# The last feed-forward part's down products in three products of rounded parts, made by ScalarE and GpSimd

## The chip, the cores and the metric

One core of a Trainium2 chip. Its engines are TensorE (PE in the profile; PEld is its weight load), VectorE (DVE), ScalarE (ACT), GpSimd (POOL) and SyncE (SP, which here only starts DMAs). The metric is the device time of one execution in microseconds, lower is better.

## The reference

A block of four layers over x (8 batches of 256 tokens, width 256): causal attention with 16 heads, a mixture of 64 experts with two shared experts, an mLSTM layer, and a feed-forward layer with 2:4 pruning. Each is `x = x + layernorm(layer(layernorm(x)))`. The change is in the last one:

```python
def _sparsify_2to4(h):                       # of each 4 neighbours the 2 of largest magnitude stay
    g = h.reshape(B, S, I // 4, 4)
    _, idx = jax.lax.top_k(jnp.abs(g), 2)
    ...
h = jax.nn.silu(x @ w_gate) * (x @ w_up)     # w_gate, w_up: 256 x 1024
return _sparsify_2to4(h) @ w_down            # w_down: 1024 x 256
```

## The kernel before

The 2048 tokens lie on 16 tiles of 128 rows. Every engine runs its own list of instructions in order, and the lists are held together by semaphores (`wait_ge`, `then_inc`); what stands behind a waiting instruction on its engine waits too. The layers follow one another, with some overlap at the borders.

The last feed-forward part works in 32 steps (`STEPS`): 4 units `u` of 512 tokens, in each 8 blocks `n` of 128 hidden columns (`NI`), i = 8u + n. The hidden columns are laid out so that the four neighbours of a pruning group fall into four blocks following each other, so pruning is done over four steps 4q to 4q+3 at a time, elementwise between whole blocks.

- TensorE, `hidden(i)`: gate and up products into PSUM banks S, 512 columns wide. The weights and the inputs are already split in rounded parts: `three` (lines 959 to 961) makes a product as high x high + high x low + low x high in the float32r type. That is 12 products a step. `down2(i)` multiplies the pruned block i with its 128 rows of w_down, four tiles of 128 tokens by 256 columns, in plain float32 (line 1518; the trace has two records for each of these). In TensorE's list `down2(i - 6)` follows `hidden(i)`. `down_last` takes the last four blocks: first two of the four token tiles for all four blocks, then the other two.
- ScalarE: `silu(i)` reads the gate bank (line 914); `magnitudes(i)` takes the absolute values (line 920). In its list step i is `magnitudes(i)`, `silu(i + 1)`.
- VectorE: `product(i)` multiplies silu and up into `hb[:, i % 8]` (line 2176). Pruning: `order_pair` (lines 2183, 2184; in the steps with i % 4 = 3 and 0), `compare_pairs` (2189, 2190; i % 4 = 0), `tallies` (2194, 2195) and the first two `sparsify` (2202) with i % 4 = 1, the last two `sparsify` with i % 4 = 2. So block 4q is pruned in step 4q+5, and TensorE multiplies it after `hidden(4q+6)`.
- The residual of a unit: in steps n = 6 and 7 of the next one `unit_stats` takes the moments from PSUM (lines 1558, 1561), `unit_residual` normalises (1566) and adds (2230), in step n = 7 for the first half and in step n = 0 of the one after for the second. The factor 1/sqrt(variance + eps) comes from GpSimd (`ln_event`, lines 446 and 447, into `veps` and `rstd`); VectorE waits for it. `last_rows` puts the output and residual of the mLSTM layer's last batch into the steps 0 to 10; it needs two more of these events, "out" for step 6 and "res" for step 8.
- GpSimd has nothing else in this part than these nine events, in a plain row.

The earlier feed-forward part (the shared experts of the mixture) already works with rounded hidden parts: ScalarE's `hidden_high` copies, rounded, GpSimd's `low_hidden` (line 466) or VectorE subtracts, and `rows_down` multiplies with `three`.

```python
for i in range(STEPS + 6):               # TensorE
    if 2 <= i < STEPS:
        hidden(i)
    ...
    if 6 <= i < STEPS + 2:
        down2(i - 6)
down_last()
```

Of the kernel before, what the change touches and what calls it, by code (L numbers as in the profile page):

```python
# [6 lines left out]
ALU = mybir.AluOpType  # L7
# [47 lines left out]
def build(nc, io, out):  # L55
    ctx = ExitStack()
    with ctx:
# [131 lines left out]
                  for i in range(2))  # L189

        lastw = parts[:, 0:NI * 2 * BW].rearrange("p (n k w) -> p n k w", n=NI, k=2)
        ordered = raw[:, :, 0:2 * KC * P]

# [246 lines left out]
        def _(pool):  # L441
            ch = Chain(pool, s["pool_c"])

            def ln_event(event, cp, n=2):
                pool.wait_ge(s["ln_mv"], event + 1)
                cp(pool.tensor_scalar(veps[:, 0:n], mv[:, 0:n, 1], LN_EPS, None, ALU.add))  # L446
                pool.tensor_tensor(rstd[:, 0:n], veps[:, 0:n], mhalf[:, 0:n], ALU.pow).then_inc(s["ln_rs"], 1)  # L447
# [171 lines left out]
                    gather_rows(b + 3, (5, 6, 7))  # L619
                    shared_row(b + 3)  # L620
            base += 4 * NB
            ln_event(ln_at["out", NB - 1], cp)
            ln_event(ln_at["res", NB - 1], cp)
            for k in range(2 * NUNIT - 1):
                ln_event(base + k, cp, 4 if k == 2 * NUNIT - 4 else 2)

        @block.scalar
        def _(act):
# [286 lines left out]
            def magnitudes(i):  # L916
# [2 lines left out]
                    act.wait_ge(s["d_cmp"], (i - 4) // 2 + 1)  # L919
                act.activation(ab[:, i % 4, :], hb[:, i % 8, :], ACT.Abs).then_inc(s["d_abs"], 1)  # L920

            silu(0)
            for i in range(STEPS):
                magnitudes(i)
                if i == 2:
                    head_rows_copy(NB)
                if i + 1 < STEPS:
                    silu(i + 1)
                if i == 9:
                    final_input_copy(NB - 1)  # L930

# [2 lines left out]
        def _(pe):  # L934
# [565 lines left out]

            def down2(i):
                u, n = divmod(i, NI)
                pe.wait_ge(s["d_hs"], i + 1)
                if i == 0:
                    pe.wait_ge(s["w_down"], 32)
                    pe.wait_ge(s["c_hc"], NB)
                if i == NI:
                    pe.wait_ge(s["c_xall"], NB + 1)
                if n == 0 and u >= 2:
                    pe.wait_ge(s["d_x"], u - 1)  # L1510
                for t in range(4):
                    last = down_tile(i, t)
                last.then_inc(s["d_dn"], 1)

            def down_tile(i, t):
                u, n = divmod(i, NI)
                bank, o = ROWS[2 * ((u + 1) % 2) + t // 2], (t % 2) * D
                last = pe.matmul(bank[:, o:o + D], hb[:, i % 8, t * P:(t + 1) * P], down_rows[n // RING][:, n % RING, :],  # L1518
                                 start=n == 0 and t % 2 == 0, stop=n == NI - 1, skip_group_check=True)
                if n == NI - 1 and t == 1:  # L1520
                    last.then_inc(s["d_half"], 1)
                return last

            def down_last():
                for half in range(2):
                    for i in range(STEPS - 4, STEPS):
                        if half == 0:
                            pe.wait_ge(s["d_hs"], i + 1)
                        for t in (2 * half, 2 * half + 1):
                            last = down_tile(i, t)  # L1530
                        if half:
                            last.then_inc(s["d_dn"], 1)
# [17 lines left out]
        def _(dve):  # L1550
# [620 lines left out]
            def product(i):  # L2171
                dve.wait_ge(s["d_sg"], i + 1)
                dve.wait_ge(s["d_u"], i + 1)
                if i >= 8:
                    dve.wait_ge(s["d_dn"], i - 7)
                dve.tensor_tensor(hb[:, i % 8, :], sgl[i % 2], S[2 + i % 2][:], ALU.mult).then_inc(s["d_h"], 1)

            def order_pair(q, p):
# [162 lines left out]
```

## Time and profile before

| | us |
|---|---|
| median of 3 runs (lowest, highest) | 975.22 (974.08, 975.96) |
| the profiled execution: span from its first to its last instruction | 1017.7 |
| TensorE busy in it | 862.2 (85%) |
| VectorE busy | 667.7 (66%) |
| GpSimd busy | 396.7 (39%) |
| ScalarE busy | 389.5 (38%) |

The profile is of one execution, and no time of it as a whole is shown beside its span; the span is 42 us above the median of the runs. Times in the rows are us from the start of the span. A timeline row gives start, duration, engine, source line, operation, output and inputs by tile name, shape, the number of instructions merged in it, and in brackets how long the engine had been idle and what ended that. The last feed-forward part lies between 848 and 1012 us.
### The profile page before, as it was taken

What the parts mean: (1) busy time and instruction counts of PE and PEld (TensorE: products, weight loads), DVE (VectorE), ACT (ScalarE), POOL (GpSimd) and SP (SyncE); (2) the same over time, 40 slices, a digit from 0 to 9 for tenths busy, and PEclk for the clock granted to TensorE, in tenths of its full rate; (3) what the DMA queues carried; (4) which work ended last, traced back from release to release, by engine and by line L of the source; (5) the groups of instructions that cost most, each with busy time, mean ns of one, the idle gap of its engine ahead of it and who ended that gap; (6) DMA issues with size and microseconds to landing.
All of it is one profiled execution on the core that took longest, in us unless ns stands there. A gap on an engine that the chain in (4) does not pass through costs nothing.

```text
span 1017.7 us, 18542 instructions
## 1 busy us (share of the span) xinstructions
PE 862.2 (85%) x6718; PEld 722.4 (71%) x6718; DVE 667.7 (66%) x1500; ACT 389.5 (38%) x764; POOL 396.7 (39%) x548
## 2 busy tenths in 40 slices
PE   4899899898688857667777859899999999999994
PEld 3777777776576846556666748778788888788883
DVE  6567777765577615885444547668778865867875
ACT  2244444444433713232222325435555564222220
POOL 3123333323432266766565283466665322100001
PEclk9799999998899968998898977758888887999997
DMA  7000000000000248888876551221111000000001
GB/s 248 2 1 13 12 12 9 5 12 12 22 1 22 87 136 260 250 257 242 242 222 184 162 178 52 82 59 52 46 42 41 0 1 1 0 1 21 22 1 41
DMA packets 59384, 77.66 MB, mean 76 GB/s; under 512 B 9746, under 2 KB 51997, under 8 KB 59304
## 3 DMA queue, kind: packets, MB, share of 16 engines
q1 hardware_dynamic: 32040, 40.92, 13.1%
q0 software_dynamic: 9856, 18.92, 6.9%
q10 hardware_dynamic: 17408, 16.78, 4.7%
q8 instruction: 47, 0.77, 0.3%
q14 instruction: 33, 0.27, 0.1%
HBM read 61.88 MB, written 23.07 MB: 83 GB/s over the span
## 4 chain that ended last, share of the span: by engine, by line
PE 43%; DVE 12%; issue 5%; another core or an unknown queue 4%; ACT 3%; POOL 2%; DMA 1%; ACTq 0%; POOLq 0%; DVEq 0%
PE S L1310 5%; PE S L1298 4%; PE S L959 3%; PE S L961 3%; PE S L960 3%; PE S L944 3%; PE ZO L1518 2%; PE ZO L1321 2%; PE T L1321 2%; PE T L1518 2%; PE ZO L1431 2%; DVE work L1566 1%; PE ZO L1433 1%; PE ZO L1432 1%
## 5 line engine op out<-in xcount | busy, mean ns | idle before, releaser
L529 POOL DMA_INDIRECT work<-xnd,rows_at x128 | 134.8, 1053 | 87.6 <-issue 38.6
L446 POOL TENSOR_SCALAR veps<-mv 128x2 f32<-128x2 f32 (+1 forms) x63 | 15.6, 247 | 287.8 <-DVE mv L1561 287.6
L1999 DVE TENSOR_TENSOR work<-work,S 64x256 f32<-64x256 f32 x128 | 54.2, 424 | 83.0 <-ACT work L798 52.9
L455 POOL TENSOR_SCALAR_AFFINE_SELECT work<-work 128x256 f32<-128x256 f32 x128 | 53.7, 444 | 118.0 <-ACT work L650 118.0
L959 PE MATMUL ZO<-parts 128*128 128x256 f32 x224 | 71.4, 319 | 16.6 <-DVE parts L1600 6.4
L959 PE MATMUL S<-xr,parts 128*128 128x512 f32 x192 | 83.5, 435 | 0.8 <-issue 0.8
L960 PE MATMUL S<-xr,parts 128*128 128x512 f32 x192 | 77.5, 404 | 0.0
L961 PE MATMUL S<-xr,parts 128*128 128x512 f32 x192 | 77.5, 403 | 0.0
L782 ACT ACTIVATE work<-S 128x512 f32<-128x512 f32 x64 | 38.2, 597 | 100.7 <-PE S L1298 43.5
L650 ACT ACTIVATE work<-S 128x768 f32<-128x768 f32 x64 | 51.7, 812 | 55.5 <-PE S L1033 55.5
L960 PE MATMUL ZO<-parts 128*128 128x256 f32 x224 | 66.3, 296 | 0.0
L961 PE MATMUL ZO<-parts 128*128 128x256 f32 x224 | 66.2, 295 | 0.0
L1033 PE MATMUL S<-parts 32*128 32x256 f32 (+1 forms) x768 | 57.9, 288 | 4.8 <-DVE parts L1626 3.8
L959 PEld LDWEIGHTS ZO<-parts 128*128 128x128 f32 x224 | 45.3, 202 | 21.9 <-issue 9.3
L1310 PE MATMUL S<-work,raw 128*128 128x128 f32 x296 | 46.7, 309 | 10.8 <-issue 10.7
L545 POOL DMA_INDIRECT attn_w<-yd,slots x44 | 49.8, 1131 | 11.9 <-issue 11.9
L1298 PE MATMUL S<-ident,work 128*128 128x128 f32 x256 | 47.4, 314 | 8.2 <-DMA work<-xnd,rows_at 8.2
L1033 PEld LDWEIGHTS S<-parts 32*128 32x128 f32 x768 | 48.9, 191 | 7.1 <-DVE parts L1626 5.0
L1310 PEld LDWEIGHTS S<-work,raw 128*128 128x128 f32 x296 | 42.5, 221 | 13.0 <-issue 12.9
L447 POOL TENSOR_TENSOR rstd<-veps,mhalf 128x2 f32<-128x2 f32 (+1 forms) x63 | 48.1, 763 | 5.2
L798 ACT ACTIVATE work<-S 64x256 f32<-64x256 f32 x64 | 24.1, 377 | 59.1 <-remote 30.8
L960 PEld LDWEIGHTS ZO<-parts 128*128 128x128 f32 x224 | 45.8, 205 | 0.1
(330 smaller groups left out, 2355.7 us busy)
## 6 DMA issues: line engine op xcount, KB each, us to landing
yd<-work ACTq DMA_DIRECT2D x64, 256.0 KB
raw<-in_experts SPq DMA_DIRECT2D x74, 192.0 KB
work<-in_experts SPq DMA_DIRECT2D x36, 192.0 KB
lg_all<-in_experts SPq DMA_DIRECT2D x18, 192.0 KB
xnd<-attn_w SPq DMA_DIRECT2D x8, 256.0 KB, 2.1
shd<-work SPq DMA_DIRECT2D x8, 256.0 KB, 2.3
work<-xnd,rows_at POOLq DMA_INDIRECT x128
raw<-in_ffn SPq DMA_DIRECT2D x2, 1024.0 KB, 5.4
```

The costliest lines, as they stand in the source:

```text
L447: pool.tensor_tensor(rstd[:, 0:n], veps[:, 0:n], mhalf[:, 0:n], ALU.pow).then_inc(s["ln_rs"], 1)
L455: last = pool.affine_select(out=diagonal, in_=diagonal, compare_op=ALU.is_ge, fill=0.0, base=0, pattern=[[0, 2], [1, P]], channel_multipli ...
L529: pool.indirect_dma_start(xg[:, i % RING, b, :], None, xnd[:], bass.IndirectOffsetOnAxis(ap=rows_at[:, 2 * i + b:2 * i + b + 1], axis=0), ...
L545: pool.indirect_dma_start(gathered(b, t, k), None, yd[:], bass.IndirectOffsetOnAxis(ap=slots[:, 2 * b + t, k:k + 1], axis=0)).then_inc(s[" ...
L650: act.activation(pt[n % 6], SS[:, at:at + 1024].rearrange("p (r x) -> p r x", r=2)[:, :, 0:384], ACT.Exp).then_inc(s["a_exp"], 1)
L959: pe.matmul(dst, a(0), b(0), start=start, stop=False, skip_group_check=True)
L960: pe.matmul(dst, a(0), b(1), start=False, stop=False, skip_group_check=True)
L961: return pe.matmul(dst, a(1), b(0), start=False, stop=stop, skip_group_check=True)
L1033: return pe.matmul(bank[:, 2 * half * P:(2 + half) * P], side, top, start=k == 0 and half == 0, stop=k == 2, skip_group_check=True)
L1298: last = pe.transpose(S[i % 2][:, o:o + P], xg[:, i % RING, b, c * P:(c + 1) * P], ident[:])
L1310: last = pe.matmul(S[2 + i % 2][:, b * P:(b + 1) * P], pair_weights(i)[:, o:o + P], xT[:, i % 2, b, c, :], start=(c == 0), stop=(c == KC - 1))
L1999: last = dve.tensor_tensor(hx[64 * half:64 * half + 64, i % 2, :], sgx[64:128, i % 2, :], S[2 + i % 2][64:128, 0:256], ALU.mult)
```

## The change

The down products are made by `three` from rounded parts, too. The parts of the eight weight blocks are made once, at the start (`down_high` on ScalarE, `down_low` on GpSimd). The parts of each pruned block are made by `kept_high` (ScalarE, a copy into float32r) and `kept_low` (GpSimd, the block less its high part), in a ring of four. TensorE waits for the low part (`f_hl`) instead of for the pruned block (`d_hs`), and VectorE's `product(i)`, which writes over block i-8, waits for the low part of that block instead of for its down product. The layer norm events on GpSimd are put between the `kept_low` of the steps.

```diff
+        last_down = lastw[:, :, :, 2 * KC * P:BW]
+        last_hidden = parts[:, NI * 2 * BW:].rearrange("p (m k t) -> p m k t", m=4, k=2)
@@ gpsimd @@
-            ln_event(ln_at["out", NB - 1], cp)
-            ln_event(ln_at["res", NB - 1], cp)
-            for k in range(2 * NUNIT - 1):
-                ln_event(base + k, cp, 4 if k == 2 * NUNIT - 4 else 2)
+            def down_low(n):
+                pool.wait_ge(s["f_wh"], NSH + NI + n + 1)
+                pool.tensor_tensor(last_down[:, n, 1], down_rows[n // RING][:, n % RING, :], last_down[:, n, 0],
+                                   ALU.subtract).then_inc(s["f_wl"], 1)
+
+            def kept_low(i):
+                pool.wait_ge(s["f_hh"], NQ * NJ + i + 1)
+                pool.tensor_tensor(last_hidden[:, i % 4, 1, :], hb[:, i % 8, :], last_hidden[:, i % 4, 0, :],
+                                   ALU.subtract).then_inc(s["f_hl"], 1)
+
+            for n in range(NI):
+                down_low(n)
+            for i in range(STEPS + 3):
+                q, j = divmod(i, 4)
+                u, n = divmod(i, NI)
+                if q and j in (1, 2):
+                    kept_low(4 * q + 2 * j - 6)
+                    kept_low(4 * q + 2 * j - 5)
+                if i == 5:
+                    ln_event(ln_at["out", NB - 1], cp)
+                if i == 6:
+                    ln_event(ln_at["res", NB - 1], cp)
+                if 0 < u < NUNIT - 1 and n >= 6:
+                    ln_event(base + 2 * (u - 1) + n - 6, cp)
+                if i == STEPS - 1:
+                    ln_event(base + 2 * (NUNIT - 2), cp, 4)
+            for k in range(2):
+                ln_event(base + 2 * NUNIT - 3 + k, cp)
@@ scalar @@
+            def down_high(n):
+                act.wait_ge(s["w_down"], 16 * (n // RING + 1))
+                act.activation(last_down[:, n, 0], down_rows[n // RING][:, n % RING, :], ACT.Copy).then_inc(s["f_wh"], 1)
+
+            def kept_high(i):
+
+                act.wait_ge(s["d_hs"], i + 1)
+                if i >= 4:
+                    act.wait_ge(s["d_dn"], i - 3)
+                act.activation(last_hidden[:, i % 4, 0, :], hb[:, i % 8, :], ACT.Copy).then_inc(s["f_hh"], 1)
+
             silu(0)
-            for i in range(STEPS):
-                magnitudes(i)
+            for i in range(STEPS + 3):
+                q, j = divmod(i, 4)
+                if i < STEPS:
+                    magnitudes(i)
                 if i == 2:
                     head_rows_copy(NB)
                 if i + 1 < STEPS:
                     silu(i + 1)
+                if i < 4:
+                    down_high(2 * i)
+                    down_high(2 * i + 1)
+                if q and j in (1, 2):
+                    kept_high(4 * q + 2 * j - 6)
+                    kept_high(4 * q + 2 * j - 5)
@@ tensor, down2 @@
-                pe.wait_ge(s["d_hs"], i + 1)
+                pe.wait_ge(s["f_hl"], NQ * NJ + i + 1)
+                if i < NI:
+                    pe.wait_ge(s["f_wl"], NSH + NI + i + 1)
@@ tensor, down_tile @@
-                last = pe.matmul(bank[:, o:o + D], hb[:, i % 8, t * P:(t + 1) * P], down_rows[n // RING][:, n % RING, :],
-                                 start=n == 0 and t % 2 == 0, stop=n == NI - 1, skip_group_check=True)
+                last = three(bank[:, o:o + D], lambda k: last_hidden[:, i % 4, k, t * P:(t + 1) * P],
+                             lambda k: last_down[:, n, k], n == 0 and t % 2 == 0, n == NI - 1)
@@ tensor, down_last @@
-                            pe.wait_ge(s["d_hs"], i + 1)
+                            pe.wait_ge(s["f_hl"], NQ * NJ + i + 1)
@@ vector, product @@
-                    dve.wait_ge(s["d_dn"], i - 7)
+                    dve.wait_ge(s["f_hl"], NQ * NJ + i - 7)
```

## Rows read from the trace of the kernel before

**Rows 1.** Busy time by stretch: us, busy (records) by engine, granted clock, DMA

```profile
870.00:980.00 110.00, 108.08 (x478) 89.11 (x477) 84.76 (x151) 29.74 (x49) 6.91 (x12) 1.00 0.03 10
```

**Rows 2.** TensorE's timeline, steps 9 to 11: start, us, engine, line, tiles, records

```profile
891.99 1.89 PE L1518 MATMUL ZO<-lg_all,work 128*128 128x256 f32 x8
896.52 1.89 PE L1518 MATMUL ZO<-lg_all,work 128*128 128x256 f32 x8
```

**Rows 3.** TensorE's timeline, earlier feed-forward part in three products

```profile
588.54 0.29 PE L959 MATMUL ZO<-parts 128*128 128x256 f32 x1
...
589.99 0.40 PE L959 MATMUL S<-xr,parts 128*128 128x512 f32 x1
...
592.79 0.28 PE L959 MATMUL ZO<-parts 128*128 128x256 f32 x1
```

**Rows 4.** Timeline of VectorE and ScalarE, steps 9 and 10

```profile
887.65 0.69 DVE L2176 TENSOR_TENSOR work<-work,S 128x512 f32<-128x512 f32 x1
...
889.58 1.29 DVE L2202 SCALAR_TENSOR_TENSOR work<-attn_w,work 128x512 f32<-128x512 bf16 x2
...
890.79 0.60 ACT L914 ACTIVATE work<-S 128x512 f32<-128x512 f32 x1 [1.79 <-PE S L961]
```

**Rows 5.** ScalarE's groups by line and shape: count, busy us, mean ns

```profile
L715 ACT ACTIVATE parts<-work 128x512 fp32r<-128x512 f32 x16 | 10.1, 632 | 25.8 <-DVE work L1736 22.6 <-issue 3.2
```

**Rows 6.** GpSimd's subtraction of the earlier part, line 466: ns minimum/median/maximum

```profile
L466 POOL TENSOR_TENSOR parts<-work,parts x12: 1262/1296/2841, 283.0 to 344.2; 128x512 fp32r<-128x512 f32 x12
```

**Rows 7.** Timeline of VectorE and GpSimd where the two meet

```profile
292.87 1.23 DVE L1773 TENSOR_TENSOR lg_all<-lg_all,work 128x1024 f32<-128x1024 f32 x1
292.97 2.27 POOL L466 TENSOR_TENSOR parts<-work,parts 128x512 fp32r<-128x512 f32 x1 [5.05 <-ACT parts L715]
294.13 2.19 DVE L1776 TENSOR_TENSOR work<-lg_all,rbias 128x1024 f32<-128x1024 f32 x1
```

**Rows 8.** GpSimd's timeline, one layer norm event of the last part

```profile
913.29 0.22 POOL L446 TENSOR_SCALAR veps<-mv 128x2 f32<-128x2 f32 x1 [34.34 <-DVE mv L1561]
913.60 0.72 POOL L447 TENSOR_TENSOR rstd<-veps,mhalf 128x2 f32<-128x2 f32 x1
```

**Rows 9.** VectorE's timeline over one unit, steps 13 to 21

```profile
905.94 0.69 DVE L2176 TENSOR_TENSOR work<-work,S 128x512 f32<-128x512 f32 x1 [0.42 <-PE S L961]
...
914.88 0.69 DVE L2176 TENSOR_TENSOR work<-work,S 128x512 f32<-128x512 f32 x1 [1.68 <-ACT work L914]
...
917.29 0.99 DVE L1566 TENSOR_SCALAR work<-ZO,mv,rstd 128x256 f32<-128x256 f32 x2
...
928.11 1.29 DVE L2202 SCALAR_TENSOR_TENSOR work<-attn_w,work 128x512 f32<-128x512 bf16 x2
...
942.87 0.69 DVE L2176 TENSOR_TENSOR work<-work,S 128x512 f32<-128x512 f32 x1 [0.41 <-PE S L961]
```

**Rows 10.** Busy time by stretch around two pauses of TensorE, with its granted clock

```profile
258.50:260.30 1.80, 0.06 (x1) 0.00 (x0) 0.44 (x1) 1.80 (x5) 1.67 (x4) 1.00 0.42 146
260.30:262.00 1.70, 1.68 (x40) 1.25 (x44) 0.00 (x0) 1.70 (x3) 1.66 (x1) 1.00 0.04 10
272.90:276.00 3.10, 0.00 (x0) 0.00 (x0) 1.89 (x8) 0.00 (x0) 0.94 (x2) 1.00 0.00 0
276.00:278.00 2.00, 1.95 (x7) 1.75 (x8) 0.76 (x2) 0.80 (x2) 0.00 (x0) 0.50 0.38 131
```

**Rows 11.** Timeline of TensorE and VectorE in the tail

```profile
996.83 10.21 PE L1518 MATMUL T<-lg_all,work 128*128 128x256 f32 x32 [2.96 <-DVE work L2202]
...
1003.62 0.76 DVE L1558 BATCH_NORM_STATS2 st<-T 128x6 f32<-128x256 f32 x2 [1.65 <-PE T L1518]
...
1007.70 0.76 DVE L1558 BATCH_NORM_STATS2 st<-T 128x6 f32<-128x256 f32 x2
```

**Rows 12.** Timeline of TensorE and VectorE, down product 0 and the last output's normalisation

```profile
873.35 1.99 PE L1518 MATMUL ZO<-raw,work 128*128 128x256 f32 x8 [0.93 <-DVE work L2202]
...
874.41 0.99 DVE L1566 TENSOR_SCALAR work<-T,mv,rstd 128x256 f32<-128x256 f32 x2
```

More of the change, by code:

```diff
@@ L1502, in down2 @@
                 u, n = divmod(i, NI)
-                pe.wait_ge(s["d_hs"], i + 1)
+                pe.wait_ge(s["f_hl"], NQ * NJ + i + 1)
+                if i < NI:
+                    pe.wait_ge(s["f_wl"], NSH + NI + i + 1)
                 if i == 0:
-                    pe.wait_ge(s["w_down"], 32)
                     pe.wait_ge(s["c_hc"], NB)
```

## Prediction

> **What bounds the kernel now.** I read the busy shares by stretch first, then TensorE's timeline, then VectorE's and ScalarE's around the places where TensorE takes up a down product. In the last feed-forward part TensorE is busy for 108.08 of 110 us, at full clock; VectorE for 84.76, ScalarE for 29.74 and GpSimd for 6.91 [rows 1]. So TensorE sets the time there, and a shorter down product would pay, if nothing new comes between. One step (hidden unit i of 32: 12 products of 512 columns for gate and up, then the down product of unit i-6) takes 896.52 - 891.99 = 4.53 us [rows 2]. The earlier feed-forward part has the changed form of the step already: 12 products of 256 columns take 589.99 - 588.54 = 1.45 us, and 12 of 512 take 592.79 - 589.99 = 2.80 us [rows 3]. So the down product costs 4.53 - 2.80 = 1.73 us now.
>
> **TensorE's gain.** The rounded form costs 1.45 us instead of 1.73: 0.28 us for each of 32 steps, 9.0 us in all, if every operand waits ready. A step becomes 4.25 us, four of them 17.0 us instead of 18.1.
>
> **The weights' parts.** Eight copies on ScalarE and eight subtractions on GpSimd, all before step 6. ScalarE is idle most of that time, so the copies cost nothing by themselves; without that cover they would be eight times less than 0.63 us. The subtractions are charged below, with the start.
>
> **The hidden units' parts.** 32 copies on ScalarE (0.63 us each, by a copy of this shape [rows 5]) and 32 subtractions on GpSimd (median 1.30 us, 1.26 to 2.84 [rows 6]). Both engines have room. What counts is where they stand in line. Units are pruned four at a time: VectorE finishes the first two in step 4q+1 and the others in step 4q+2, and TensorE wants the first one right after the 12 wide products of step 4q+2. In step 10 the pruned unit is there at 890.2 (889.58 and half of 1.29), TensorE takes it at 891.99. But ScalarE's new copy stands behind the silu of step 10, which runs from 890.79 to 891.39 [rows 4], 0.60 us before TensorE is free. Then 0.63 of copy, 0.07 to signal, 1.30 of subtraction, 0.07 to signal: 2.07 us after the silu, so TensorE waits 2.07 - 0.60 = 1.47 us. Once in four steps, in each group of four: 1.47 lost against 4 x 0.28 = 1.12 gained. The quiet groups lose 0.35 us each. The other three units have a whole step more and are ready. The wait for the ring of four, and VectorE's own (now for the subtraction instead of the down product), have long been met.
>
> **Contention.** At 292.97 a GpSimd subtraction meets a VectorE instruction with two SBUF inputs (292.87, 1.23 us) and takes 2.27 instead of 1.30; VectorE's next one, of the same size and kind, takes 2.19 instead of 1.23 [rows 7]. Each kept the other out for its whole length. All the pruning on VectorE is of this kind; its products of silu and up read PSUM and don't count. I therefore let a subtraction and a pruning instruction exclude each other; the other bound is that they don't. The Trainium skill, "SBUF — State Buffer", section "SBUF: two separate sides", states the same as a rule: the pair of ports is locked by the one that starts first, and the other blocks fully. By that rule the sum is the one with exclusion, and it speaks against this change; the trace agrees in the two instructions just read.
>
> **The groups with the layer norm.** In the last two steps of a unit of 8 (n = 6, 7) VectorE takes the moments of the unit before and waits for GpSimd's rstd, which is 0.22 + 0.72 us and some 1.0 us in all [rows 8]. The diff puts that event behind both subtractions of step n = 6. In the time of step 13's end of the wide products = 0: step 14's wait ends at 5.7, step 15's wide products at 9.95; ScalarE's silu of step 15 ends at 9.3, its two copies at 9.95 and 10.5, the subtractions run 10.0 to 11.3 and 11.3 to 12.6, or the second behind VectorE's ordering. VectorE's product is done at 10.8, but its three ordering instructions can't begin before 11.3 to 12.6 and take 1.9; rstd is there by 14.5 to 15.4. So the normalisation begins 4.3 to 5.2 us after the product's start at 10.2, where now it begins 917.29 - 914.88 = 2.4 after it [rows 9]. From there to the first pruned unit of the next group it is 928.11 + 0.65 - 917.29 = 11.5 us of VectorE's own work: 26.0 to 26.9. Copy, subtraction and signals: 28.0 to 28.9. TensorE's own work would bring it there at 0 + 5 x 4.25 + 1.47 = 22.7, so it waits 5.3 to 6.2 us. Eight steps then take 8 x 4.25 + 1.47 + 5.3 to 6.2 = 40.8 to 41.7 us, against 942.87 - 905.94 = 36.9 now: **3.9 to 4.8 us more, twice**. Without exclusion rstd is there at 13.6 and it is 2.9 more.
>
> **The clock.** A pause of 1.8 us left the granted clock at 1.00; after one of 3.1 us it was 0.50 through the 2 us that followed [rows 10], half of 2.4 GHz. The waits of 1.47 us should cost nothing more, those of 5 to 6 us should be followed by a stretch at half clock, on the path, since VectorE is ahead by then. Its price: at least 1.0 us (2 us at half speed), at most 3.3 (in the tail the first 16 of 32 records after a pause of 2.96 took 1003.62 - 996.83 = 6.79 us, the other 16 some 3.4 [rows 11]). I take 2.2, between them: **4.4 us for two**.
>
> **The start.** The weights' subtractions (half as wide as the hidden ones, by my estimate some 0.7 us each, from the 1.30 of [rows 6]) meet VectorE's ordering in steps 3 and 4 and hold it up by about the length of one, 0.65 us; copy, subtraction and signals add 2.0: down product 0 begins at 873.35 + 2.65 = 876.0. VectorE's normalisation of the last mLSTM output, at 874.41 now [rows 12], waits for a rstd that stands behind two subtractions: 876.0 + 1.3 + 0.95 = 878.2, 3.8 later. The next two subtractions hold the ordering of step 7 up for one more, and TensorE, paused for 3.6 us, is at half clock. I bring the product of step 9 to 892.4 instead of 887.65 [rows 4], the pruned unit to 895.0, down product 4 to 897.0 instead of 891.99: 5.0 us, or 4.3 without exclusion. Until step 13 three short down products and the shorter way to the product give 0.95 back: **3.4 to 4.1 us**.
>
> **The tail.** Nothing covers it. The last four units' copies and subtractions (4 x 1.3) stand behind the last pruning; TensorE's first half of the last down product ends 26.0 to 26.7 us after the wide products of step 29, where now it is 1003.62 - 979.6 = 24.0 [rows 11] (step 29 is one unit of 36.9 us after step 21, whose product starts at 942.87 [rows 9], 0.25 after its wide products). The second half is short again and the moments follow the normalisation, 1007.70 - 1003.62 = 4.1 later as now. **2.0 to 2.7 us**. VectorE's two older normalisations fit into the waiting.
>
> **The sum.** 3.8 + 2 x 4.3 + 4.4 + 2.3 = 19.1 us. The gain of 9.0 us is in it. Ends of the bounds: 3.4 + 5.8 + 2.0 + 1.5 = 12.7 with no exclusion and the smallest clock price; 4.1 + 9.6 + 6.6 + 2.7 = 23.0 with everything. The profiled execution has a span of 1017.7 us, the runs a median of 975.22: it is 42 us longer, and the trace doesn't say where. The stage repeats the same step evenly at full clock, so I carry the difference over unscaled: 975.2 + 19.1 = 994.3. Scaled by 975/1018 it would be 18.3.
>
> **Rivals.**
> 1. The forecast: waits, exclusion and clock, 15 to 23 us slower, 990 to 998. Chance 0.60.
> 2. Milder: the engines don't exclude each other or the clock stays up. 3.4 + 5.8 + 1.5 = 10.7 with neither, 19.1 - 4.4 = 14.7 with exclusion alone: 986 to 990. For it: only one meeting in the trace is unambiguous. Chance 0.20.
> 3. Harsher: a subtraction doesn't get in between VectorE's back-to-back instructions and takes 2.3 to 2.84 us, as two of 12 did [rows 6, 7]. About 1 us more in each of 7 groups: 998 to 1004. Against it: where VectorE waits for its own result there is a gap. Chance 0.10.
> 4. The other side: the way from silu to the low part is short enough. It decides at one place, copy plus subtraction behind the silu of step 4q+2: if they take less than 0.6 us instead of 2.07, TensorE never waits and keeps 9.0 us, less some 2 at the tail: 968. At 1.7 us it breaks even in the quiet groups. For it speaks only that GpSimd and ScalarE are mostly idle. Chance 0.05; that things cancel within 0.2% (about what a measurement of this kernel can tell from no change), 0.03.
>
> Slower by more than that: 0.60 + 0.20 + 0.10, and 0.02 for worse than rival 3: 0.92. Range for 8 in 10: 984 to 1002, from the lower end of the milder case to the middle of the harsher one.
>
> **What the changed profile would show.** Twelve records of 0.12 us in the place of eight of 0.216 in each down product. TensorE idle some 1.5 us before the first down product of a quiet group, released by GpSimd's subtraction; 5 to 6 us after the first steps of units 2 and 3, with a granted clock of 0.5 behind it. VectorE's ordering instructions stretched where a subtraction runs, its normalisation waiting for rstd. If TensorE's idle time before down products stays under 1 us, the forecast is wrong; if it is idle but at full clock, the clock term is; if the subtractions stay at 1.3 us and the ordering at 0.6, exclusion is.

## The result and the profile after

Four runs of the changed kernel took 992.98 us in the median (989.08 to 996.22), four of the kernel before 974.65 (973.73 to 975.96): ratio 1.0196, 95% interval 1.0159 to 1.0233. The change makes it 18.3 us slower; 994.3 in all and 19.1 more were forecast. The profiled execution took 991.72 us, with a span of 990.0.

The last part was 158.03 us long and is 176.74, from VectorE's `product(0)` to the end of its last residual addition. This table gives that time for all kernels of this study, cut at the products of steps 13, 21 and 29, each read from the starts of that instruction in VectorE's timeline. Runs of one kernel spread by up to 6 us either way. Much of that lies ahead of the last part: but for the 853.57 us of before, its first product starts anywhere from 803.08 to 816.38 us in these traces. The stretches of the table repeat to 0.1 us in many places where the work is the same (the first one of after, e2, e3 and e6, the units of e8, e12 and e13), so the verdicts below rest on them, and the runs stand beside. But where TensorE pauses for about 2 us or more, and its clock may fall, they do not all repeat so well: the two units, 13 to 21 and 21 to 29, hold the same work, and differ by 0.51 us in after, 0.86 in e3, 2.01 in e7 and 1.51 in e9. There is one trace of each kernel, so a difference of up to 2 us in such a unit or in the tail is not by itself the work of an edit. The last column compares with runs of the kernel before that were taken beside that kernel's, with medians of 973.87 to 974.66 us for the experiments.

| kernel | 0 to 13 | 13 to 21 | 21 to 29 | 29 to end | sum | runs, median | ratio to before, 95% interval |
|---|---|---|---|---|---|---|---|
| before | 52.37 | 36.93 | 36.97 | 31.76 | 158.03 | 974.65 | |
| after | 55.44 | 43.25 | 43.76 | 34.29 | 176.74 | 992.98 | 1.0159 to 1.0233 |
| e1_ready | 54.04 | 35.52 | 35.54 | 29.68 | 154.78 | 972.90 | 0.9966 to 1.0016 |
| e2_fill | 55.45 | 41.06 | 41.07 | 34.37 | 171.95 | 987.99 | 1.0106 to 1.0193 |
| e3_ln_first | 55.44 | 42.72 | 41.86 | 35.10 | 175.12 | 991.68 | 1.0117 to 1.0206 |
| e4_low_on_vector | 52.66 | 41.66 | 41.35 | 34.49 | 170.16 | 987.47 | 1.0084 to 1.0155 |
| e5_low_last | 54.29 | 40.82 | 40.89 | 33.20 | 169.20 | 986.97 | 1.0116 to 1.0179 |
| e6_residual_late | 55.45 | 41.89 | 42.46 | 35.99 | 175.79 | 991.12 | 1.0140 to 1.0216 |
| e7_all | 52.29 | 40.21 | 38.20 | 33.60 | 164.30 | 981.21 | 1.0051 to 1.0103 |
| e8_before_residual_late | 52.32 | 36.20 | 36.22 | 30.40 | 155.14 | 971.53 | 0.9956 to 1.0002 |
| e9_high_first | 52.28 | 38.26 | 39.77 | 32.69 | 163.00 | 979.25 | 1.0036 to 1.0078 |
| e10_ready_residual_late | 54.03 | 33.95 | 33.92 | 29.65 | 151.55 | 968.99 | 0.9929 to 0.9974 |
| e12_before_late_fill | 52.33 | 36.21 | 36.21 | 30.25 | 155.00 | 972.88 | 0.9943 to 0.9991 |
| e13_before_tail_order | 52.32 | 36.20 | 36.21 | 29.39 | 154.12 | 968.83 | 0.9931 to 0.9983 |

The first view of the kernel after is busy time by stretch; its last part begins at 807.17, where that of before began at 853.57, so the first stretch is the one of [rows 1], moved by 46.4 us. Engines stand in the order PE, PEld, DVE, ACT, POOL, then the granted clock. The second row lies behind a pause of 1.15 us (first down product of a quiet group, at 911.04), the last two behind the pause of 5.44 us at 890.45.

```profile
823.60:933.60 110.00, 92.70 (x495) 78.55 (x493) 90.81 (x139) 38.47 (x66) 37.86 (x33) 0.95 0.03 10
...
911.00:913.00 2.00, 1.96 (x14) 1.91 (x15) 2.00 (x2) 0.34 (x1) 1.70 (x1) 1.00 0.00 0
...
890.40:894.50 4.10, 4.05 (x16) 3.76 (x17) 2.23 (x2) 0.00 (x0) 1.69 (x1) 0.50 0.00 0
894.50:897.00 2.50, 2.50 (x10) 2.00 (x9) 0.00 (x0) 1.19 (x3) 0.00 (x0) 0.81 0.00 0
```

TensorE was busy for 108.08 of 110 us and is for 92.70: it no longer sets the time. Its timeline names who does. In it, 867.79 is the first down product of a quiet group, 890.45 and 933.72 the first after a unit's layer norm, 829.09 the very first and 969.77 the last four blocks'.

```profile
829.09 0.39 PE L1004 MATMUL ZO<-parts 128*128 128x256 f32 x1 [3.07 <-POOL parts L631]
...
866.25 0.39 PE L1006 MATMUL S<-xr,parts 128*128 128x512 f32 x1
867.79 0.39 PE L1004 MATMUL T<-parts 128*128 128x256 f32 x1 [1.15 <-POOL parts L631]
...
872.13 0.28 PE L1004 MATMUL T<-parts 128*128 128x256 f32 x1
...
873.57 0.40 PE L1004 MATMUL S<-xr,parts 128*128 128x512 f32 x1
...
890.45 0.58 PE L1004 MATMUL T<-parts 128*128 128x256 f32 x1 [5.44 <-POOL parts L631]
...
933.72 0.58 PE L1004 MATMUL ZO<-parts 128*128 128x256 f32 x1 [5.45 <-POOL parts L631]
...
969.77 0.58 PE L1004 MATMUL T<-parts 128*128 128x256 f32 x1 [6.14 <-POOL parts L631]
```

L631 is `kept_low`'s subtraction. Where nothing is late, the down product takes 873.57 - 872.13 = 1.44 us (1.73 before, [rows 2, 3]). Next ScalarE (L940 silu, L957 `kept_high`), GpSimd and VectorE around the quiet group's wait, the places of [rows 4 to 6]:

```profile
865.28 0.60 ACT L940 ACTIVATE work<-S 128x512 f32<-128x512 f32 x1 [1.32 <-PE S L1006]
865.77 1.14 ACT L957 ACTIVATE parts<-work 128x512 fp32r<-128x512 f32 x2
...
866.47 2.97 POOL L631 TENSOR_TENSOR parts<-work,parts 128x512 fp32r<-128x512 f32 x2 [9.72 <-ACT parts L957]
...
864.53 1.29 DVE L2248 SCALAR_TENSOR_TENSOR work<-attn_w,work 128x512 f32<-128x512 bf16 x2
866.73 0.69 DVE L2222 TENSOR_TENSOR work<-work,S 128x512 f32<-128x512 f32 x1 [0.91 <-ACT work L940]
867.34 2.65 DVE L2248 SCALAR_TENSOR_TENSOR work<-attn_w,work 128x512 f32<-128x512 bf16 x2
```

The reader sees two things. The copies run right behind the silu, and the subtraction behind them. And the two pruning instructions at 867.34, which meet the two subtractions, take 2.65 us where the two at 864.53 took 1.29; the two subtractions take 2.97 where a pair that met no such instruction (827.76) took 2.51. From the first start to the last end the four take 867.34 + 2.65 - 866.47 = 3.52 us, hardly less than 2.51 + 1.29 = 3.80: the two engines work nearly one after the other. Last, VectorE and GpSimd in step 15, the place of [rows 8, 9]:

```profile
872.39 0.69 DVE L2222 TENSOR_TENSOR work<-work,S 128x512 f32<-128x512 f32 x1 [1.44 <-ACT work L940]
872.99 2.68 DVE L2229 TENSOR_TENSOR raw<-attn_w 128x512 f32<-128x512 f32 x2
875.60 0.68 DVE L2230 TENSOR_TENSOR attn_w<-attn_w 128x512 bf16<-128x512 f32 x1
876.89 0.99 DVE L1612 TENSOR_SCALAR work<-ZO,mv,rstd 128x256 f32<-128x256 f32 x2 [0.61 <-POOL rstd L449]
...
872.12 3.00 POOL L631 TENSOR_TENSOR parts<-work,parts 128x512 fp32r<-128x512 f32 x2 [2.68 <-ACT parts L957]
875.09 0.66 POOL L448 TENSOR_SCALAR veps<-mv 128x2 f32<-128x2 f32 x1
875.84 1.01 POOL L449 TENSOR_TENSOR rstd<-veps,mhalf 128x2 f32<-128x2 f32 x1
```

The normalisation begins 876.89 - 872.39 = 4.50 us after the product, where it was 2.4. In the tail VectorE's moments answer to [rows 11]: the second ones again 4.07 us behind the first, and these 975.93 - 949.62 = 26.3 us behind the product of step 29.

```profile
975.93 0.76 DVE L1604 BATCH_NORM_STATS2 st<-T 128x6 f32<-128x256 f32 x2 [2.21 <-PE T L1006]
...
980.00 0.76 DVE L1604 BATCH_NORM_STATS2 st<-T 128x6 f32<-128x256 f32 x2
```

### The profile page after: what moved, and what is told of

Same layout as the page of the kernel before. It is cut to its first block, busy times and chain, and to the rows that moved or that the text cites. A ratio compares the mean times of both kernels' runs of the same rounds, so it can differ in the third digit from the quotient of the medians.

```text
span 990.0 us, 18913 instructions
## 1 busy us (share of the span) xinstructions
PE 835.5 (84%) x6846; PEld 704.6 (71%) x6846; DVE 687.1 (69%) x1500; ACT 409.8 (41%) x804; POOL 449.5 (45%) x588
## 4 chain that ended last, share of the span: by engine, by line
PE 31%; DVE 15%; POOL 10%; issue 8%; DMA 4%; ACT 3%; POOLq 0%; DVEq 0%; ACTq 0%
DMA work<-xnd,rows_at 4%; POOL work L531 3%; PE S L989 3%; PE S L1004 3%; PE S L1005 3%; PE S L1006 3%; POOL parts L631 2%; DVE work L1612 2%; PE S L1355 2%; DVE st L1604 2%; PE S L1343 2%; POOL attn_w L547 1%; DVE attn_w L2008 1%; DVE work L2121 1%; PE T L1427 1%
## 5 line engine op out<-in xcount | busy, mean ns | idle before, releaser
L1004 PE MATMUL ZO<-parts 128*128 128x256 f32 x288 | 90.6, 315 | 26.5 <-POOL parts L631 10.8
L631 POOL TENSOR_TENSOR parts<-work,parts 128x512 fp32r<-128x512 f32 x32 | 47.2, 1499 | 91.4 <-ACT parts L957 91.4
L1005 PE MATMUL ZO<-parts 128*128 128x256 f32 x288 | 84.9, 295 | 0.0
L1006 PE MATMUL ZO<-parts 128*128 128x256 f32 x288 | 84.7, 294 | 0.0
L1004 PEld LDWEIGHTS ZO<-parts 128*128 128x128 f32 x288 | 58.0, 201 | 34.0 <-POOL parts L631 12.6
L1343 PE MATMUL S<-ident,work 128*128 128x128 f32 x256 | 44.3, 298 | 24.6 <-DMA work<-xnd,rows_at 24.4
L1005 PEld LDWEIGHTS ZO<-parts 128*128 128x128 f32 x288 | 58.6, 203 | 0.6
L1006 PEld LDWEIGHTS ZO<-parts 128*128 128x128 f32 x288 | 58.6, 203 | 0.0
L1343 PEld LDWEIGHTS S<-ident,work 128*128 128x128 f32 x256 | 28.6, 147 | 34.3 <-DMA work<-xnd,rows_at 22.3
```

Source lines behind the costliest of these rows:

```text
L631: pool.tensor_tensor(last_hidden[:, i % 4, 1, :], hb[:, i % 8, :], last_hidden[:, i % 4, 0, :], ALU.subtract).then_inc(s["f_hl"], 1)
L1004: pe.matmul(dst, a(0), b(0), start=start, stop=False, skip_group_check=True)
L1005: pe.matmul(dst, a(0), b(1), start=False, stop=False, skip_group_check=True)
L1006: return pe.matmul(dst, a(1), b(0), start=False, stop=stop, skip_group_check=True)
L1343: last = pe.transpose(S[i % 2][:, o:o + P], xg[:, i % RING, b, c * P:(c + 1) * P], ident[:])
```

## The experiments

**e1_ready: the short down product alone.** Only the first four blocks are split; all later ones are multiplied with the parts of these four, as soon as their own pruned block is there. Its result is another one; its time is that of the short product without the copies, subtractions and their waits.

```diff
-                if q and j in (1, 2):
+                if q == 1 and j in (1, 2):
@@ tensor, down2 @@
-                pe.wait_ge(s["f_hl"], NQ * NJ + i + 1)
+                pe.wait_ge(s["d_hs"], i + 1)
+                pe.wait_ge(s["f_hl"], NQ * NJ + min(i + 1, 4))
...
```

> Changed kernel, but only the first four pruned blocks are split in high and low parts; all down products from block 4 on multiply those four again (so the result is another), and TensorE waits for the pruned block as before. The 28 copies on ScalarE and 28 subtractions on GpSimd are gone; TensorE's instructions are those of the changed kernel. Theory (the loss is the waits for copy and subtraction, with exclusion and clock): faster than the kernel before by some 3 us, about 972: a unit of 8 steps takes 35.4 us (VectorE's pruning chain is next in line and eats the rest of the gain), 36.9 before, 43.5 in the changed kernel. Rival A (the whole 9 us of TensorE's gain comes out once operands are ready): 966 to 968. Rival B (the three products, their weight loads or the rounded operands cost it by themselves): stays above 985.

Last part 154.78 us: 22.0 less than after, 3.3 less than before. So all the loss is the supply of the parts. But of TensorE's 9.0 us only a third comes out. The start, where the first four blocks are still split, is 1.7 us longer than before. And the trace names who keeps the most in the units: one takes 35.52 and not 8 x 4.25 = 34.0, and once in each TensorE waits for VectorE's pruning (L2249 here).

```profile
886.70 0.39 PE L1004 MATMUL T<-parts 128*128 128x256 f32 x1 [1.35 <-DVE work L2249]
```

**e2_fill: the clock term.** The waits stay as they are, but 22 products with an unused result fill TensorE's pause in the unit steps.

```diff
+                    if 16 < i < STEPS and i % NI == 2:
+                        pe.wait_ge(s["d_sg"], i)
+                        for k in range(22):
+                            pe.matmul(S[(i + 1) % 2][:], lastw[:, 0, 0, 0:P], xr[:, 0, 0, 0:512], start=True, stop=True)
```

> Changed kernel plus 22 more products of 512 columns (5.1 us at full clock) on TensorE ahead of the down products of steps 18 and 26, where it is idle for 5.4 us; they write a bank that the next step clears. Theory (the clock falls during the idle time and costs 2.2 us each behind it): 4 to 5 us faster than the changed kernel, 988 to 989, granted clock 1.00 behind both places, a unit in 41.2 us instead of 43.5. Rival (VectorE and GpSimd set the time there, the clock of TensorE is hidden): 993, unit unchanged.

The units take 41.06 and 41.07 instead of 43.25 and 43.76: 2.19 and 2.69 us less, the other stretches are unchanged. The stretches behind the filled pause are at full clock:

```profile
886.00:891.00 5.00, 5.00 (x23) 3.85 (x21) 4.72 (x8) 2.63 (x5) 0.80 (x1) 1.00 0.31 105
891.00:893.00 2.00, 1.67 (x13) 1.46 (x13) 2.00 (x2) 0.33 (x1) 2.00 (x2) 1.00 0.00 0
```

The clock term is shown, and with it the rest of the unit's time: 41.06 was forecast as 40.8 to 41.7. In the runs the kernel takes 987.99 us, as expected.

**e3_ln_first: the order on GpSimd.** The layer norm event stands ahead of the step's two subtractions, not behind them (the `kept_low` lines of the loop move below the `ln_event` lines).

> Changed kernel with each layer norm event on GpSimd ahead of the subtractions of its step instead of behind them. Theory: the 3.1 us that VectorE waits for rstd in step 6 go, of which some 2.5 us reach the end, and 0.6 us for each of two units: 989. Rival (VectorE is held by the exclusion anyway, the order doesn't matter): 992 to 993.

Only 1.6 us less (0.5 and 1.9 in the two units, 0.8 more in the tail, of which the clock's part isn't known), and the start not at all: 55.44 as before the edit. The normalisation behind product(15) now begins 874.72 - 870.91 = 3.81 us after it, not 4.50, and the unit's pause shrinks from 5.44 to 4.75. In step 6 VectorE no longer waits for rstd, and yet product(7) comes 7.69 us after product(6), as after the change:

```profile
826.06 0.68 DVE L2222 TENSOR_TENSOR work<-work,S 128x512 f32<-128x512 f32 x1
826.66 0.99 DVE L1612 TENSOR_SCALAR work<-T,mv,rstd 128x256 f32<-128x256 f32 x2
827.69 1.66 DVE L2106 TENSOR_TENSOR x_sb<-x_sb,work 128x512 f32<-128x512 f32 x1
...
833.75 0.69 DVE L2222 TENSOR_TENSOR work<-work,S 128x512 f32<-128x512 f32 x1 [2.15 <-PE S L1006]
```

The 3 us that VectorE saves turn into a wait for TensorE, which has the pause of 3.07 us before its first down product and is slow behind it. The theory had that wait on the path; it was second in line.

**e4_low_on_vector: no subtractions on GpSimd in this part's steps.** VectorE makes the low parts itself, one step apart from ScalarE's copies; GpSimd keeps the events and the weights' parts.

```diff
@@ vector, step i @@
+                if j == 2 and q:
+                    kept_low(i - 6)
...
+                    kept_low(i - 5)
+                if j == 3 and q:
+                    kept_low(i - 5)
+                    kept_low(i - 4)
...
```

> Changed kernel with the 32 low parts of the hidden blocks made by VectorE (0.6 us each) instead of GpSimd (1.3 to 1.5). Theory (GpSimd's length and the exclusion cost more than VectorE's own 0.6 us): the quiet wait of 1.3 us becomes 0.7, the unit's wait 4.0 instead of 5.6, the tail 1.5 shorter: 983 to 985. Rival (32 more instructions make VectorE the bound): 993 or more.

6.6 us less than after. VectorE's subtraction takes 0.69 us where GpSimd's took 1.27 to 1.79 and kept VectorE out meanwhile; the pause of a quiet group is 0.54. Whether the length or the exclusion matters more, this run doesn't tell, as it takes away both. With 987.47 us it misses the 983 to 985 that were expected. The tail, where 1.5 us less had been expected, is 0.2 longer, and in the units the subtractions now stand in the pruning's own line:

```profile
887.01 0.69 DVE L2274 TENSOR_TENSOR parts<-work,parts 128x512 fp32r<-128x512 f32 x1
887.62 0.68 DVE L2214 TENSOR_TENSOR work<-work,S 128x512 f32<-128x512 f32 x1
...
887.75 0.58 PE L996 MATMUL T<-parts 128*128 128x256 f32 x1 [3.95 <-DVE parts L2274]
```

**e5_low_last: TensorE asks for the low part last.** A down product makes its eight products with the high part first and waits for `f_hl` only before the other four.

```diff
-                pe.wait_ge(s["f_hl"], NQ * NJ + i + 1)
+                pe.wait_ge(s["f_hh"], NQ * NJ + i + 1)
...
+                for t in tiles:
+                    for k in range(2):
+                        pe.matmul(at(t), part(0, t), last_down[:, n, k], start=n == 0 and t % 2 == 0 and k == 0,
...
+                pe.wait_ge(s["f_hl"], NQ * NJ + i + 1)
+                for t in tiles:
+                    last = pe.matmul(at(t), part(1, t), last_down[:, n, 0], start=False, stop=n == NI - 1,
...
```

> Changed kernel with the 12 products of a down block in another order: the 8 that need only the high hidden part first (TensorE waits for the copy), then the 4 with the low part (it waits for the subtraction). Theory (what TensorE waits for is the low part, 1.3 us behind the high one): 8 products of 0.12 us lie under the subtraction, so each of the waits of steps 10, 14, 18, 22, 26, 30 is 1.0 us shorter and the start and the tail 1 us each: 985. Rival (VectorE and GpSimd set the pace and TensorE only shows it): 992 to 993.

7.5 us less, in every stretch. The subtraction's 1.3 us now run beside the eight products, and what is left is the copy's line:

```profile
827.45 1.21 PE L1572 MATMUL ZO<-parts 128*128 128x256 f32 x8 [1.72 <-ACT parts L957]
828.82 0.75 PE L1577 MATMUL ZO<-parts 128*128 128x256 f32 x4 [0.15 <-POOL parts L631]
...
886.75 2.07 PE L1572 MATMUL T<-parts 128*128 128x256 f32 x8 [4.11 <-ACT parts L957]
```

**e6_residual_late and e8_before_residual_late: the residual's place.** In both, the second half of a unit's residual moves from step n = 0 to n = 3, in the changed kernel and in the kernel before.

```diff
-                if u > 1 and n == 0 and u < NUNIT:
+                if u > 1 and n == 3 and u < NUNIT:
                     unit_residual(u - 2, 1)
```

> Changed kernel with VectorE's normalisation and residual of the second half of a unit in step n = 3 instead of n = 0. Theory (VectorE's chain sets the long wait of step n = 2): that chain is 1.9 us shorter, twice: 989. Rival (TensorE's own rate or GpSimd sets it): 993.

> The kernel before with only the second half's residual moved to step n = 3. Theory: takes away the 0.7 us by which a unit exceeds eight steps: 973.3. Rival: no difference.

The kernel before gets 2.9 us shorter: 0.7 in each unit and 1.4 in the tail. The changed one only 0.95: its unit's pause shrinks by the residual's length, but the quiet group behind it has less room, and its pause grows from 1.15 to 2.08; and the tail gets 1.7 us longer (35.99). About 1.0 of that comes ahead of the last four down products: behind the pause of 1.79 at 951.29 the clock fell, to 0.89 over the first 2 us and to 0.50 after that. The rest comes with the last products, at half clock for longer.

```profile
888.12 0.58 PE L1004 MATMUL T<-parts 128*128 128x256 f32 x1 [3.49 <-POOL parts L631]
...
908.82 0.39 PE L1004 MATMUL ZO<-parts 128*128 128x256 f32 x1 [2.08 <-POOL parts L631]
```

**e7_all: the edits of e3, e5 and e6 together.**

> Changed kernel with three of these together: layer norm events ahead of the subtractions, products with the low part last, the second half's residual in step n = 3. Theory: the savings add up, 3.8 + 8 + 3.8 = 15 us, with some clock given back: 975 to 979. Rival: they shorten the same wait and don't add: 985.

164.30 us, 12.4 less than after; the three alone gave 1.6, 7.5 and 0.95, 10.1 in all. The 2.3 more come mostly in the start, which is 52.29, as before: e3's order alone gave nothing there and e5's 1.15, both give 3.15. With TensorE's pause cut to 1.72 (e5) the wait for rstd is first in line: e5's trace still has it, and e7_all's does not.

```profile
831.04 1.00 DVE L1624 TENSOR_SCALAR work<-T,mv,rstd 128x256 f32<-128x256 f32 x2 [3.10 <-POOL rstd L449]
```

The sum of 12.4 misses the 15 that were expected, and the 981.21 us of the runs the 975 to 979. It remains 9.2 us slower than e8, which has the same residual and plain products.

**e9_high_first: the copy ahead of the silu.** e7_all, and ScalarE copies the first block of each group before the silu of its step.

```diff
+                if q and j == 1:
+                    kept_high(4 * q - 4)
@@ behind the silu @@
-                    kept_high(4 * q + 2 * j - 6)
+                    if j == 2:
+                        kept_high(4 * q + 2 * j - 6)
```

> The kernel of e7_all, and besides ScalarE's copy of the first block of each group of four now stands ahead of the silu of that step, not behind it (0.60 us). What e7_all still lost in a quiet group was a TensorE pause of 1.72 to 2.30 us before the first down product. Theory (the line behind the silu is what TensorE waits for, and nothing else has moved in yet): the pauses of the quiet groups shrink by up to 0.60 us, those of the unit steps and the tail hardly at all, so the last part gets 1.5 to 2.5 us shorter than e7_all's 164.3 us: 162 to 163 us, and the run at about 979. Rival A (the copy's early place delays the silu by 0.6 us, VectorE's product waits for that silu, and everything comes as late as before): 164 to 165 us, run 981 as e7_all. Rival B (VectorE's pruning chain bounds the rounded form anyway): 164 us too, but with TensorE's pauses ended by VectorE's product, not by ScalarE or GpSimd.

163.00 us and 979.25 in the runs, as the theory has it, but hardly by its mechanism. The expectation had the pauses in the wrong place: in e7_all those of 1.72, 2.30 and 2.24 us stand at the start and in the unit steps, and the later quiet groups have 0.59 and 0.72. In e9 they are 1.73, 2.25, 2.23, 0.72 and 0.74: none got shorter by the 0.60. The early copy shows in one place, a step whose down product waited for its low part (4.72 us from 872.54 in e7_all, 4.24 from 863.38 in e9).

The two units together are 0.38 us shorter: the first by 1.95, the second longer by 1.57, because a pause of 2.2 us was followed by half clock in the first unit of e7_all and in the second of e9. The tail is 0.91 shorter; there the two traces agree to 0.02 us until 22.4 us behind the product of step 29, when the clock comes back in e9, and some 6 us later in e7_all. So what the edit is worth lies near 0.4 us, and the rest is the clock, which can fall out either way. The same pause with full clock behind it and with half clock, first in e9, then in e7_all:

```profile
882.70:884.00 1.30, 1.22 (x8) 1.02 (x8) 0.79 (x2) 1.06 (x3) 1.24 (x1) 1.00 0.00 0
884.00:886.00 2.00, 1.89 (x10) 1.66 (x11) 2.00 (x2) 0.56 (x1) 1.76 (x2) 1.00 0.00 0
...
921.00:922.30 1.30, 1.18 (x8) 0.97 (x8) 0.87 (x2) 1.06 (x3) 1.30 (x2) 1.00 0.00 0
922.30:924.30 2.00, 1.97 (x7) 1.77 (x8) 2.00 (x2) 0.48 (x1) 1.66 (x1) 0.55 0.00 0
```

```profile
893.70:895.70 2.00, 1.89 (x7) 1.69 (x8) 2.00 (x2) 0.00 (x0) 1.75 (x2) 0.60 0.00 0
...
933.30:935.30 2.00, 1.85 (x10) 1.63 (x11) 2.00 (x2) 0.00 (x0) 1.80 (x2) 1.00 0.00 0
```

**e10_ready_residual_late: the short product with ready parts.** e1_ready with the residual of e8.

> The kernel of e1_ready (only the first four blocks are split, all others take these four blocks' parts, so its result is another one: what is left is the time of the short down products with their parts always there), with the residual of a unit's second half in step n = 3 instead of n = 0, as in e8_before_residual_late. Theory (with ready operands VectorE's own pruning chain bounds the unit steps, pauses 1.35 us ended by VectorE): the move takes that pause away, 2.9 us as it did for the kernel before (158.0 to 155.1), so the last part takes about 151.8 us instead of 154.8, which is the ceiling of what the rounded form could give: some 3.3 us better than the kernel before with the same move; run about 969. Rival (the pause of e1_ready comes from something else than VectorE's line): 154.8 us, run 972.

151.55 us. TensorE waits for nothing in the units, which take 33.95: eight steps of 4.24. So the short product is worth 3.6 us against e8 if its operands are always ready: 2.3 in each unit and 0.75 in the tail, less 1.7 in the start, where the first four blocks are still split. It is not quite the ceiling: e7_all's order of the same split work brings the start down to 52.29, and with that the gain would be some 5.3 us, an estimate from this sum.

**e12_before_late_fill and e13_before_tail_order: the tail of the kernel before.** Both keep plain products and e8's residual. e12 fills TensorE's pause of 2.96 us with 12 products whose result isn't used; e13 besides takes the last unit's first moments ahead of the second older residual.

```diff
+            pe.wait_ge(s["d_sg"], STEPS - 1)
+            for k in range(12):
+                pe.matmul(S[0][:], lastw[:, 0, 0, 0:P], xr[:, 0, 0, 0:512], start=True, stop=True)
             down_last()
@@ e13 besides, vector @@
-            for k in range(2):
-                unit_residual(NUNIT - 2, k)
+            unit_residual(NUNIT - 2, 0)
             unit_stats(NUNIT - 1, 0)
+            unit_residual(NUNIT - 2, 1)
```

> The kernel before with plain float32 down products and the late residual of e8_before_residual_late, and besides 12 products of 512 columns into a free bank of TensorE ahead of the last down products, so that TensorE isn't idle in the tail; their result isn't used. Theory (a pause of 2.96 us in the tail is followed by half clock on the path, worth some 2 us there): the end comes 1.2 to 2.0 us earlier, the last part takes 153.1 to 153.9 us instead of 155.1, run about 970. Rival (the fillers end after VectorE's last pruned block is there, or the clock falls nevertheless): 155.1 to 156 us, run 971.5 to 973.

> The kernel of e12_before_late_fill, and besides VectorE takes the moments of the last unit's first half before the second of the two older residuals, not after it. In e12's trace TensorE kept its full clock in the tail, but the moments began at 957.08, right behind VectorE's second older residual (955.21 to 956.93), while the first half of the products was done by about 955.7: so the gain of the clock went into VectorE's line. Theory: the moments begin about 1.4 us earlier, the older residual fills the wait for rstd (1.16 us) and overruns it by some 0.5, so the end comes 0.8 us earlier: from the product of step 29 to the end 29.4 to 29.6 us instead of 30.25, the last part 154.2 us, run about 0.8 us under e12's and within the measurement of it. Rival (the first half of the products is not done before 957, as the trace merges their records): 30.2 us or more, up to 30.8 as the older residual then delays the normalisation.

e12 ends only 0.15 us earlier than e8, not 1.2 to 2.0. The clock did stay up, and the 32 last products run from 951.78 for 7.17 us instead of 8.86. But VectorE is next, and takes the moments right behind its older residual:

```profile
955.21 0.99 DVE L1569 TENSOR_SCALAR work<-ZO,mv,rstd 128x256 f32<-128x256 f32 x2
956.24 0.69 DVE L2233 TENSOR_TENSOR x_sb<-x_sb,work 128x512 f32<-128x512 f32 x1
957.08 0.76 DVE L1561 BATCH_NORM_STATS2 st<-T 128x6 f32<-128x256 f32 x2
```

e13 gives the 0.86 us that were expected of its order (29.39). With 154.12 us for the last part and 968.83 in the runs, 0.9931 to 0.9983 of before, it is the fastest kernel with a right result here; it has nothing of the change in it. That its runs lie 4 us below e12's is more than the 0.9 of the last part, and within their spread (964 to 976 for e12, 967 to 976 for e13).

## Why the prediction was right

The likeliest case came true, by its own steps; the terms follow in the order of the forecast.

- **TensorE's gain**, 0.28 us a step: 1.73 to 1.44, and 4.24 a step in e10. Right, but it needs more than ready parts: e1 shows VectorE's pruning 1.35 us late in each unit even then.
- **The quiet wait**, forecast 1.47: the wide products end at 866.25 + 0.23 = 866.48, the down product starts at 867.79, 1.31 us. The silu ended 0.60 us before, as forecast (865.88); of the difference of 0.16, 0.11 is that the copy's record starts before the silu's ends (865.77). The 1.15 in the row counts from the end of the last wide product's record, 866.25 + 0.40.
- **Exclusion**: right. Where two subtractions run, two pruning or ordering instructions take 2.65 to 3.14 us on VectorE instead of 1.29. The trace of the changed kernel agrees with the Trainium skill, "SBUF — State Buffer", section "SBUF: two separate sides", which has the pair of ports locked by the one that starts first. At 867.34 VectorE lost 1.36 us, about one subtraction, and GpSimd 0.46; such losses fit engines that take turns, instruction by instruction. They speak against the harsher rival, in which GpSimd would have waited for the whole pair. The four instructions took 0.28 us less than one after the other would, so the exclusion is not quite of the whole length; and what it costs by itself, no run tells.
- **The groups with the layer norm**, forecast 3.9 to 4.8 without the clock: e2 gives 41.06 - 36.93 = 4.13. The normalisation's 4.50 us lay in the 4.3 to 5.2.
- **The clock**, forecast 2.2 each: 2.19 and 2.69 by e2. None after the pauses of 1.15. That it fits so well is partly luck: the forecast took the middle between 1.0 and 3.3, and the units of one trace differ by up to 2.0 us where the clock is in play.
- **The start**, forecast 3.4 to 4.1: 3.07. Two terms were off. Down product 0 came 2.14 us later (829.09 - 807.17 against 873.35 - 853.57), not 2.65: the weights' subtractions stretched the ordering by 0.20 and 0.43 us (816.60 and 819.40), but the pruning behind it came only 0.12 later, as VectorE had idle time between. Down product 4 was then 3.83 us later (849.42 - 807.17 against 891.99 - 853.57), not 5.0. And the wait for the mLSTM output's rstd, which the forecast put on the path, was hidden behind TensorE's pause: e3 took it away and nothing moved.
- **The tail**, forecast 2.3: 2.53.
- **The sum**: 3.07 + 6.32 + 6.79 + 2.53 = 18.7, forecast 3.8 + 4.3 + 4.3 + 4.4 + 2.3 = 19.1. The 42 us by which the profiled execution of before was longer lay ahead of the last part in all but a fraction: product(0) started at 853.57 there and at 807.17 here. To carry the difference over unscaled was right. Two slips of the working changed nothing here: the 1.5 us for the tail in the lower bound is worked out nowhere, and the range starts at 984 where the milder case that it names starts at 986.

What the forecast did not have: that the waits stand one behind the other, so that undoing them one by one does not add up (e3 gave nothing at the start alone, 2.0 us together with e5). No order of the same work that was tried here comes within 0.2% of the kernel before; e9 is the nearest, 0.6% above it. And e10 shows that the change had little to win even with ready parts, 3.6 us against e8. Nor was TensorE the whole bound before: moving one residual of VectorE's took 2.9 us off the kernel before (e8).

## What to carry to other kernels

A faster instruction is worth its saving only if its operand is there at once, so count the hand-overs that the new form needs between the last instruction of the old supply and the first of the new use, and the lines that these stand in; here 2 us of them, of which 1.31 stay uncovered once in four steps, outweigh four savings of 0.28, and the units, each with one group behind a layer norm, lose 6.3 to 6.8 us with the clock. Make the products that need the latest operand last: that alone gave 7.5 of 18.7 us back. And after taking away a wait, look for what is second in line at the same place, before crediting it with its length (e3, e12).

## What the runs showed of the hardware that was not expected

- Around 2 us the length of TensorE's pause did not decide what its clock did. Pauses of 2.24 (e7) and 2.25 us (e9) left it at 1.00; those of 2.30 (e7) and 2.23 (e9) were followed by half clock from about 1.5 us after the restart, and the step behind took 6.29 us instead of 4.75. Pauses of 1.15, 1.72 (e4, e5, e7), 1.95 (e5), 2.08 (e6) and even 2.44 (e4) left it at 1.00, and one of 1.79 (e6) did not. Behind all of 2.96 and more the products started at half clock or fell to it. What decides stays open.
- A half-rate clock need not cost its time: in e12 the last products got 1.69 us shorter and the end came 0.15 earlier, as VectorE was next in line.
- GpSimd's small instructions for rstd take longer as well while VectorE works on two inputs from SBUF: 0.66 and 1.01 us at 875.09, against 0.22 and 0.72 [rows 8].
